# Attention and gated FFN layer on 8 cores: loading the second half of the sequence by casting DMAs, ahead of the projections

## Reference, cut to what matters

```python
x = L0_attn_x                                   # (4, 2048, 2048) float32
xn = (x - mean(x)) / sqrt(var(x) + 1e-5)        # over the last axis
Q, K = relu(xn @ Wq.T + bq), relu(xn @ Wk.T + bk)   # 16 heads of 128
V = xn @ Wv.T + bv
Q, K = Q * decay, K * decay                     # decay = exp(-pos / n)
KV = einsum('bhnd,bhne->bhde', K, V)            # summed over the whole sequence
Z = 1 / (einsum('bhnd,bhd->bhn', Q, K.sum(axis=2)) + 1e-6)
s = (einsum('bhnd,bhde->bhne', Q, KV) * Z) @ Wo.T + bo
g = silu(layernorm(xn) @ sign(W).T * max(abs(W)) * gamma + beta)
return x + s * g
```

## Time and profile before

| | |
|---|---|
| time, 3 runs | median 1334.43 us (1330.36 to 1335.74) |
| profiled execution: time, span of its slowest core | 1341.13 us, 1339.6 us (core 5) |
| spans of the 8 cores | 1325.4 to 1339.6 us |
| granted clock of TensorE, mean of a core | 0.892 to 0.898 |
| busy share of core 5 | PE 73%, DVE 25%, ACT 20%, POOL 17% |

### The profile page before, as it was taken

How to read it: one execution, slowest core, us unless ns; L and a number is a source line. 1 busy time by engine, 2 the same in 40 slices (tenths; PEclk the granted TensorE clock), 3 DMA queues, 4 the chain that set the end, 5 groups by cost and what they waited for, 6 DMA issues and landing times.

```text
span 1339.6 us, 15619 instructions; the slowest of 8 cores (1325.4 to 1339.6 us)
## 1 busy us (share of the span) xinstructions
PE 982.7 (73%) x4433; PEld 429.3 (32%) x4433; DVE 336.1 (25%) x673; ACT 274.3 (20%) x407; POOL 224.5 (17%) x250
## 2 busy tenths in 40 slices
PE   0000552464999999999999999999444599989774
PEld 0000221122443444344444444444222244433332
DVE  1446234323002000200000004000666445523233
ACT  1233112321111111111111111222223222271000
POOL 3000000000015500481000000441700200013320
PEclk9999965776998999899999999999555699988888
DMA  9942112210026000804000002873000675459975
GB/s 154 180 95 78 48 32 63 63 32 17 1 38 89 0 1 0 126 4 45 1 0 1 1 1 47 79 75 37 1 1 1 89 158 148 125 95 173 150 137 154
DMA packets 141296, 85.07 MB, mean 64 GB/s; under 512 B 71408, under 2 KB 137120, under 8 KB 141216
## 3 DMA queue, kind: packets, MB, share of 16 engines
q0 software_dynamic: 84672, 33.58, 22.5%
q1 hardware_dynamic: 48096, 42.10, 10.8%
q10 hardware_dynamic: 8448, 8.39, 2.2%
HBM read 109.22 MB, written 8.40 MB: 88 GB/s over the span
## 4 chain that ended last, share of the span: by engine, by line
PE 60%; DMA 16%; DVE 13%; issue 5%; ACT 4%; DVEq 1%; SPq 1%; ACTq 0%; POOL 0%; POOLq 0%
PE pb L579 17%; PE pb L598 17%; PE pb L706 8%; PE pb L822 7%; DMA xres<-xT 7%; DMA xf<-xq 5%; DVE otile L776 3%; DMA xf<-xoq 3%; DVE s L370 2%; DVE s L366 2%; DVE outF L895 2%; PE pb L603 2%; PE pb L584 2%; ACT xbf L339 1%; PE pb L558 1%
## 5 line engine op out<-in xcount | busy, mean ns | idle before, releaser
L579 PE MATMUL pb<-WkB,xbf 128*128 128x512 bf16 x1024 | 244.9, 395 | 0.2 <-PE pb L442 0.2
L598 PE MATMUL pb<-WvB,xbf 128*128 128x512 bf16 x1024 | 232.1, 380 | 0.1
L380 PE MATMUL pb<-onescf,s 128*128 128x1 f32 x32 | 8.9, 348 | 223.8 <-DVE s L366 222.5
L880 PE MATMUL pb<-outT,WcolO 128*128 128x512 bf16 x512 | 123.0, 406 | 23.5 <-DVE outF L887 20.7
L579 PEld LDWEIGHTS pb<-WkB,xbf 128*128 128x128 bf16 x1024 | 100.5, 101 | 120.9 <-issue 22.8
L598 PEld LDWEIGHTS pb<-WvB,xbf 128*128 128x128 bf16 x1024 | 94.9, 98 | 120.4 <-issue 14.7
L822 PE MATMUL pb<-xn2T,SgB 128*128 128x512 bf16 x512 | 115.0, 388 | 8.6 <-ACT SgB L811 8.6
L706 PE MATMUL pb<-xn_own,Wcol 128*128 128x512 bf16 x512 | 110.7, 379 | 2.1 <-DVE KVbf L635 2.1
L590 ACT ACTIVATE Ktile<-pb,grd 128x512 bf16<-128x512 f32 x64 | 44.1, 689 | 309.2 <-PE pb L584 270.2
L178 POOL DMA_DIRECT2D WcolO<-woT x64 | 47.6, 768 | 283.9 <-PE pb L880 202.9
L178 POOL DMA_DIRECT2D Wcol<-wqT x64 | 47.7, 770 | 268.8 <-PE pb L706 268.8
(11 more groups left out here) (91 smaller groups left out, 728.0 us busy)
## 6 DMA issues: line engine op xcount, KB each, us to landing
WsB<-wsT SPq DMA_DIRECT2D x64, 256.0 KB, 3.9
WkB<-wkT POOLq DMA_DIRECT2D x16, 512.0 KB, 13.4
WvB<-wvT POOLq DMA_DIRECT2D x16, 512.0 KB, 23.4
Wcol<-wqT POOLq DMA_DIRECT2D x64, 128.0 KB, 3.9
WcolO<-woT POOLq DMA_DIRECT2D x64, 128.0 KB, 6.4
xres<-xT SPq DMA_DIRECT2D x16, 512.0 KB, 5.6
yT<-outF SPq DMA_DIRECT2D x16, 512.0 KB, 3.4
xf<-xq SPq DMA_DIRECT2D x8, 512.0 KB, 7.9
```

The source lines that it names most:

```text
L579: te(lambda E, kc=kc, kb=kb, tc=tc, p=p: E.matmul(out=pb[kb][:, 0:DTILE], lhsT=xbf[:, kc * SEQ + tc * 128:kc * SEQ + tc * 128 + 128], rhs= ...
L598: te(lambda E, kc=kc, vb=vb, tc=tc, p=p: E.matmul(out=pb[vb][:, 0:DTILE], lhsT=xbf[:, kc * SEQ + tc * 128:kc * SEQ + tc * 128 + 128], rhs= ...
L880: dP = te(lambda E, kc=kc, bi=bi, b3=b3, tt=tt: E.matmul(out=pb[bi][:, 0:NT], lhsT=WcolO[b3][:, kc * 128:(kc + 1) * 128], rhs=outT[:, kc * ...
```

## The change

The other half of x is no longer loaded into `xf` and cast by ACT. Sixteen DMAs on POOL's queue, with a cast from float32 to bf16, write it straight into `xbf`. They stand behind the column sums of the weights, ahead of the loop over `dt`, and count on the semaphore `gx1`. In the loop `emit_oth_stats` takes the place of `emit_slab2` for the other half: it has the same squares, the same DVE sums and the same matmuls, and no load and no cast. `d_sl[tc]` of the other half is now the list of these DMAs instead of the casts.

```diff
         flush_half(0)
         emit_wsum(0, 2, 3)
 
+        d_xoth = {}
+        for q in range(NQ):
+            for pl in range(TC // 2):
+                blk = (q * (TOWN // 256) + pl) * KCq * 128
+                d_xoth[(q, pl)] = dma(
+                    "gpsimd",
+                    xbf[:, :].rearrange("p (kc t) -> p kc t", t=SEQ)[
+                        :, q * KCq:(q + 1) * KCq,
+                        TOWN + pl * 256:TOWN + (pl + 1) * 256],
+                    ap["xoq"][blk:blk + KCq * 128, :].rearrange(
+                        "(kc p) t -> p kc t", p=128), "gx1")
+        for sg in range(TC, 2 * TC):
+            pl = (sg % TC) // 2
+            d_sl[sg] = [d_xoth[(q, pl)] for q in range(NQ)]
+
+        def emit_oth_stats(ps, bmA, bmB):
...
+            for q in range(NQ):
+                dQ = sc(lambda E, q=q, scolA=scolA: E.activation(
+                    out=xsq[:, :].rearrange("p (kc t) -> p kc t", t=256),
...
+                    func=AF.Square),
+                    deps=sq_r[0].users + [d_xoth[(q, pl)]])
+                sq_r[0].users = []
+                for k2 in range(KCq):
...
+                        d1 = ve(lambda E, xsl=xsl: E.tensor_copy(
+                            out=s1[:, :], in_=xsl),
+                            deps=[d_xoth[(q, pl)]] + prev_su)
...
+                        d1 = ve(lambda E, xsl=xsl: E.tensor_tensor(
+                            out=s1[:, :], in0=s1[:, :], in1=xsl, op=ALU.add),
+                            deps=[d_xoth[(q, pl)], d1])
+                        d2 = ve(lambda E, k2=k2: E.tensor_tensor(
+                            out=s2[:, :], in0=s2[:, :],
+                            in1=xsq[:, k2 * 256:(k2 + 1) * 256], op=ALU.add),
+                            deps=[dQ, d2])
...
         for dt in range(NDT):
...
                 if dt == 0 and own_side:
                     if tc % 2 == 0:
-                        emit_slab2((TC + tc) // 2, kb, vb)
+                        emit_oth_stats(tc // 2, kb, vb)
                     if tc == TC - 1:
                         flush_half(1)
```

More of the change, by code:

```diff
@@ new lines, in build_program @@
+        for sg in range(TC, 2 * TC):
+            pl = (sg % TC) // 2
+            d_sl[sg] = [d_xoth[(q, pl)] for q in range(NQ)]
+        def emit_oth_stats(ps, bmA, bmB):
+            pl = ps % (TC // 2)
+            scolA = TOWN + pl * 256
+            off = 2 * TC
+            d1 = d2 = None
+            for q in range(NQ):
+                dQ = sc(lambda E, q=q, scolA=scolA: E.activation(
+                    out=xsq[:, :].rearrange("p (kc t) -> p kc t", t=256),
+                    in_=xbf[:, :].rearrange("p (kc t) -> p kc t", t=SEQ)[
+                        :, q * KCq:(q + 1) * KCq, scolA:scolA + 256],
+                    func=AF.Square),
+                    deps=sq_r[0].users + [d_xoth[(q, pl)]])
+                sq_r[0].users = []
+                for k2 in range(KCq):
+                    kc = q * KCq + k2
+                    xsl = xbf[:, kc * SEQ + scolA:kc * SEQ + scolA + 256]
+                    first = (q == 0 and k2 == 0)
+                    if first:
+                        prev_su = s_r.users
+                        s_r.users = []
+                        d1 = ve(lambda E, xsl=xsl: E.tensor_copy(
+                            out=s1[:, :], in_=xsl),
+                            deps=[d_xoth[(q, pl)]] + prev_su)
+                        d2 = ve(lambda E, k2=k2: E.tensor_copy(
+                            out=s2[:, :], in_=xsq[:, k2 * 256:(k2 + 1) * 256]),
+                            deps=[dQ] + prev_su)
+                    else:
+                        d1 = ve(lambda E, xsl=xsl: E.tensor_tensor(
[5 more added lines that the diff above has]
+                            deps=[dQ, d2])
+                sq_r[0].users.append(d2)
+            for sub in range(2):
+                sg = 2 * ps + sub
+                sl = sg % TC
+                bank_take(bmA)
+                dM = te(lambda E, sub=sub, bmA=bmA: E.matmul(
+                    out=pb[bmA][:, 0:1],
+                    lhsT=s1[:, sub * 128:(sub + 1) * 128],
+                    rhs=onescf[:, :], start=True, stop=True),
+                    deps=[d1, d_ones])
+                bank_prod(bmA, dM)
+                bank_take(bmB)
+                dS = te(lambda E, sub=sub, bmB=bmB: E.matmul(
+                    out=pb[bmB][:, 1:2],
+                    lhsT=s2[:, sub * 128:(sub + 1) * 128],
+                    rhs=onescf[:, :], start=True, stop=True),
+                    deps=[d2])
+                bank_prod(bmB, dS)
+                dEm = ve(lambda E, sl=sl, bmA=bmA: E.tensor_copy(
+                    out=sacc[:, off + sl:off + sl + 1], in_=pb[bmA][:, 0:1]),
+                    deps=[dM])
+                bank_use(bmA, dEm)
+                dEs = ve(lambda E, sl=sl, bmB=bmB: E.tensor_copy(
+                    out=sacc[:, off + TC + sl:off + TC + sl + 1], in_=pb[bmB][:, 1:2]),
+                    deps=[dS])
+                bank_use(bmB, dEs)
+                s_r.users += [dM, dS]
+                if sl == TC - 1:
+                    last_evac[1] = dEs
```

## The result

The changed kernel takes 1345.76 us (median of 10 runs), the kernel before 1332.63 us (median of 10): a ratio of 1.0089, 95% interval 1.0069 to 1.0110. It is slower by 9 to 15 us, and lies inside the range that was given; the forecast was 1.0052. A few runs in which the cores of a whole die had a lower clock are left out of the ratio.

What follows compares the result with a forecast made beforehand. The prediction took PE's unhidden waits at L380 for DVE's slab sums as the bound; +12.3 (first slab) - 11.3 (other three) + 6.0 (tc 8) = +7.0 us, giving 1341.4 us against 1334.43, range 1333 to 1350 us.

Steps and rivals of the forecast that it cites:

- What bounds it: Projection loop: PE waits at L380 for DVE's sums, 96 us over four slabs; nothing hides these waits.
- Removed: loads and casts: Other half's slabs: without loads and casts inside, the last three slabs gain 11.3 us in sum.
- Added: one wait for all sixteen: First slab of the loop: its squares wait for all 16 loads, landing at 175.1 us, a loss of 12.3 us.
- the fixed 1.8: Fixed part of a transfer: small DMAs of the same queue take 1.8 us to land.
- the straight line: Casting loads: a 1 KB row costs 57 ns, between 34 ns for 512 B and 102 ns for 2 KB.
- The rule on pieces under 512 B: Casting loads: if read-modify-write penalises smaller pieces, a row costs 51 ns, loads take 26.1 us, sum 3.0 us lower.
- Moved: the wait of `tc` 8: K matmuls of tc 8 wait on gx1 behind the lhsT2 DMAs, laid bare: +6.0 us, bounds 3.6 and 7.
- Sum: Whole kernel: +12.3 - 11.3 + 6.0 = +7.0 us on the profiled execution's 1341.13 us.
- Quicker loads: Rival at the 16 loads: they take 24.6 us, sum +2.5 us, no change within 0.5%; chance 0.17.
- Dear rows: Rival at the 16 loads: 1 KB rows cost 102 ns, landing at 198, sum +30, 1364 us; chance 0.14.
- mild form: Milder dear rows: 70 ns a row, sum +13.7, 1348 us; half of that rival's 0.14.
- Faster: Rival: loads land under the first chunk, all four slabs gain, -9.2 us, 1325 us; chance 0.07.

Runs made afterwards that it cites:

- the run that took the slab out of PE's way: Changed kernel with loads slab by slab on four semaphores, lhsT2 DMAs off tc 8's wait, and each slab's PE part two chunks later (one for the last): ratio 0.9417, 1252.10 us.
- the one with both edits: Changed kernel with loads issued slab by slab on four semaphores, and only the two rows' matmul waiting for lhsT2: ratio 0.9931 to the kernel before.
- The run with SP's loads: Kernel before, with SP issuing all four loads of each slab of the other half instead of ACT issuing the second and fourth: ratio 0.9929.
- the run with the old order: Changed kernel with four semaphores, one per slab, but loads still issued quarter by quarter; tc 8's wait kept: first stretch 53.5 us, single time 1343.17 us.
- The wider loads: Changed kernel with the same bytes from unsliced xoT, in 8 loads of 512 tokens or 4 of 1024: single times 1334.70 and 1333.24 us.
- the last run: Kernel before with SP issuing all loads of the other half's slabs and their PE part two chunks later, without casting loads: ratio 0.9391, 1247.89 us.

## Why the prediction was right

**What bounds it.** Held. Each change of a slab moved the end, and the run that took the slab out of PE's way gained 5% over the one with both edits (0.9417 against 0.9931).

**Removed: loads and casts, -11.3 us for three slabs.** Held: 148.8 to 137.5 us. That it is right to the digit is luck. As means over the cores, the three slabs themselves, from the first cast or squares to PE's sums, fell from 23.7, 23.3 and 23.2 to 19.8, 20.0 and 19.8 us, which is 10.7 us; 0.6 us came from between the slabs, which the prediction took as unchanged. A slab takes 19.75 us where 19.50 were reckoned. What the prediction did not do is divide the gain between the load waits and the casts. The run with SP's loads did: about three quarters are waits for loads issued late (2.6 of 3.6 us in the first slab, 7.8 of 10.7 us in the other three).

**Added: one wait for all sixteen, +12.3 us.** The mechanism held: with a semaphore for each slab and the loads in the order of use, the loss is gone. The size was too low: +15.8 us. The first squares come 19.4 us later instead of the 16.3 forecast, and the slab gains 3.6 us, not 3.95. The term that was off is the price of a row of 1 KB, 57 ns; with 33.8 us from the first issue to the squares (32.8 to 36.2 on the eight cores), less the fixed 1.8, it is 62.5 ns. Most of this is not the straight line but its two ends. The prediction took them from the time at which the bytes had moved, 28.0 and 14.9 us, while a wait is for the landing, and in the same trace (core 5 of the kernel before) the last of the eight weight loads landed at 422.6 and the last of the twelve `Wcol` loads at 616.0, 29.3 and 15.7 us behind their first issues. The same straight line through these gives 60 ns and 32.5 us, 1.3 us short of the measured. The wider loads cost 109 ns for a row of 2 KB and 213 ns for one of 4 KB.

The prediction did not mention the order of the issues. It says that the squares wait for all sixteen loads instead of their own four, which is right, but with a semaphore for each slab alone they would still have waited for the 13th: the run with the old order got back 3.9 of 19.3 us.

**The rule on pieces under 512 B.** The Trainium skill, page "DMA: Bandwidth & Descriptors", section "Specifications", says that pieces under 512 B are written by read-modify-write. My estimate for a row without that cost was 51 ns, half the price of a 2 KB row. The measured 62.5 ns is farther from that than from my straight line, so no relief for reaching 512 B shows here.

**Moved: the wait of `tc` 8, +6.0 us.** Held, at +5.2 us, and shown by the run that took it away. The matmuls took 5.47 us, most of them at half clock, not 6.0.

**Sum.** +7.0 us forecast, +9.8 in the stage, 9 to 15 us in the times. From the first to the second it is +3.5 at the first slab, most of it the later landing, and -0.8 at `tc` 8. The rest lies outside the stage. As a mean over the cores the profiled spans grow by 10.4 us (1330.1 to 1340.4), and the parts are: 1.0 us less up to the own transpose, 9.8 more in the stage, 1.3 less from there to the next column sums (142.3 instead of 143.6 us), 0.2 less in the slice after that, 1.7 more from the last column sums to the first eviction of Q (143.4 instead of 141.7), and 1.4 more from there to the end. In this last part, of some 504 us, the cores of one trace differ by 8 to 13 us, so that the slowest core's time can't be closed to a microsecond; what moves it there stays open.

**The rivals.** Quicker loads: no. Dear rows: nearly half-way to their mild form, 62.5 ns between my 57 and its 70. By the time alone, which moved by 0.89% or some 12 us, the mild form (+13.7) fits better than the forecast (+7.0); in the stage (+9.8) the forecast is the nearer one. Faster: no.

## What to carry to other kernels

A wait that counts everything issued so far on a semaphore turns each new use of that semaphore into a wait for all of its users: give each buffer that is consumed by itself its own, and issue in the order of use. Before replacing work by a special transfer, look at who issues the transfer that it replaces; here two loads of each slab, issued by an engine with nothing else to do instead of by the consumer behind its own work, were worth about as much. And a helper chain that an engine stands behind is better moved than shortened: the change with its two mends gave 0.7% against the kernel before, two chunks of distance gave some 5% more.

## What was not expected of the hardware

The same gap at the same place is followed by a lower clock in one kernel and not in the other. Ahead of the first Q matmuls PE stands 2.12 us on six cores of the kernel before, and on four cores of the changed one. The first lines are core 0 of the kernel before, the second core 3 of the changed kernel, each with two windows behind the gap:

```profile
821.91 18.29 PE L706 MATMUL pb<-xn_own,Wcol 128*128 128x512 bf16 x84 [2.12 <-DVE KVbf L635]
...
821.00:823.00 2.00, 1.09 (x6) 0.53 (x7) 0.71 (x3) 0.00 (x0) 0.00 (x0) 1.00 0.03 7
823.00:825.00 2.00, 2.00 (x11) 0.94 (x10) 1.90 (x2) 0.00 (x0) 0.00 (x0) 1.00 0.97 277
```

```profile
829.46 20.84 PE L785 MATMUL pb<-xn_own,Wcol 128*128 128x512 bf16 x88 [2.12 <-DVE KVbf L714]
...
829.00:831.00 2.00, 1.54 (x7) 0.71 (x8) 0.82 (x1) 0.00 (x0) 0.00 (x0) 0.89 0.27 80
831.00:833.00 2.00, 2.00 (x6) 0.65 (x5) 1.90 (x2) 0.00 (x0) 0.00 (x0) 0.50 0.86 217
```

In the one the granted clock stays at 1.00; in the other it falls to 0.5, and from the first Q matmul to the first eviction it is 5.45 us instead of 3.77. The clock stays up on all eight cores of the kernel before and of the one with SP's loads, whose gaps are 2.12 us and, on two cores each, 2.33 to 2.34. It falls on all eight cores of the changed kernel (2.12 to 2.40 us) and of every other run with casting loads of x (2.12 to 2.83 us). In the last run, which has no casting loads of x, it falls on four of eight, at gaps of 2.12 and of 2.33 us. So neither the length of this gap nor the casting loads as such decide it. What does was not tried.
